# A graph-attention kernel: a second tile for drained products, spreading in nine groups, and another order of loads at each layer's start

## What is computed

```python
f_ni, f_nj, f_fij = nf @ W_ni, nf @ W_nj, ef @ W_fij
f_out = leaky_relu(f_ni[src] + f_nj[dst] + f_fij + bias, 0.2).reshape(-1, H, D)
e = einsum('ehd,hd->eh', f_out, attn)
emax = segment_max(e, dst)
a = exp(e - emax[dst]); a = a / segment_sum(a, dst)[dst]
h = (nf @ W_node).reshape(-1, H, D)
h_out = segment_sum(h[src] * a[:, :, None], dst)
nf, ef = h_out.mean(axis=1), f_out.mean(axis=1)
```

## Time and profile before

| | us |
|---|---|
| median of three runs | 3715.75 |
| lowest and highest run | 3714.92, 3718.35 |
| the profiled execution, its own time | 3716.28 |
| its span, first to last instruction | 3714.5 |
| PE busy | 2692.3 (72%) |
| DVE busy | 2424.4 (65%) |
| POOL busy | 1891.6 (51%) |
| ACT busy | 1634.7 (44%) |

### The profile page before, as it was taken

The page is one execution under the profiler, slowest core; times in us unless marked ns, Lnnn a source line. Parts: engine busy times, 40 slices in busy tenths (PEclk is TensorE's granted clock), DMA queues, the critical chain, the costliest instruction groups (busy, mean ns, idle before and its releaser), DMA issues.

```text
span 3714.5 us, 54737 instructions
## 1 busy us (share of the span) xinstructions
PE 2692.3 (72%) x18232; PEld 2153.1 (58%) x18259; DVE 2424.4 (65%) x5843; ACT 1634.7 (44%) x4133; POOL 1891.6 (51%) x1987
## 2 busy tenths in 40 slices
PE   3477777768677458777777777856777787777885
PEld 2465656656565256566666656536666666666653
DVE  6376767767768536676676767753667576676775
ACT  0144544544445315454454545532444444444453
POOL 5544554554553266455554545446555454554543
PEclk8787777777879778787777878868777777777776
DMA  6244334434342334343434433233343333433322
GB/s 218 86 122 137 120 122 144 128 126 133 122 130 88 121 107 119 115 137 114 147 120 134 126 115 122 98 107 110 100 121 119 112 108 105 123 114 114 95 81 84
DMA packets 149064, 440.48 MB, mean 119 GB/s; under 512 B 40892, under 2 KB 80672, under 8 KB 129977
## 3 DMA queue, kind: packets, MB, share of 16 engines
q1 hardware_dynamic: 82746, 385.31, 29.4%
q0 software_dynamic: 63200, 36.75, 7.1%
q10 hardware_dynamic: 2838, 14.91, 1.0%
HBM read 191.89 MB, written 244.95 MB: 118 GB/s over the span
## 4 chain that ended last, share of the span: by engine, by line
DVE 36%; PE 36%; issue 13%; ACT 9%; DMA 4%; POOL 2%; DVEq 0%; ACTq 0%; SPq 0%; POOLq 0%
DVE U L1465 15%; PE pick_ps L732 14%; PE f_ps L764 11%; PE f_ps L773 5%; DVE U L1450 4%; ACT f_low L919 4%; DVE rows L1386 4%; PE xT_ps L754 4%; DVE lr L1397 4%; DVE rows L1491 3%; ACT xT L910 2%; DMA z<-hot_tab 1%; ACT pick_sb L973 1%; DVE z L1477 1%; DVE mx_sc L1421 1%
## 5 line engine op out<-in xcount | busy, mean ns | idle before, releaser
L615 POOL DMA_INDIRECT rows<-nf_tab,src_sb x1815 | 1721.8, 949 | 1505.0 <-PE xT_ps L754 669.6
L732 PE MATMUL pick_ps<-nf_part,z 125*128 125x160 bf16 x9045 | 926.1, 270 | 578.9 <-ACT pick_sb L973 446.4
L732 PEld LDWEIGHTS pick_ps<-nf_part,z 125*128 125x128 bf16 x9045 | 835.1, 115 | 624.4 <-issue 459.9
L1397 DVE TENSOR_TENSOR lr<-f_ps,f_low 128x512 f32<-128x512 f32 x606 | 413.3, 682 | 930.7 <-ACT f_low L919 930.5
L773 PEld LDWEIGHTS f_ps<-w_out,lr 128*128 128x128 f32 x4836 | 721.4, 215 | 396.4 <-issue 296.7
L764 PE MATMUL f_ps<-xT,w_edge 97*128 97x512 f32 x1212 | 804.5, 752 | 70.2 <-ACT ef_new L941 47.2
L1465 DVE TENSOR_TENSOR_SCAN U<-wide_ps,U 128x272 f32<-128x272 f32 (+2 forms) x1272 | 801.9, 694 | 3.0 <-ACT wide_ps L982 1.9
L773 PE MATMUL f_ps<-w_out,lr 128*128 128x36 f32 (+1 forms) x4836 | 663.7, 278 | 30.2 <-DVE lr L1397 27.8
L919 ACT ACTIVATE f_low<-f_ps 128x512 f32<-128x512 f32 x606 | 360.6, 595 | 652.8 <-PE f_ps L764 652.5
L754 PE MATMUL xT_ps<-ident,rows 128*97 128x128 f32 x2418 | 449.9, 314 | 170.9 <-DVE rows L1386 141.8
L754 PEld LDWEIGHTS xT_ps<-ident,rows 128*97 128x97 f32 x2418 | 330.0, 186 | 188.5 <-DVE rows L1386 146.9
(11 more groups left out here) (164 smaller groups left out, 1215.4 us busy)
## 6 DMA issues: line engine op xcount, KB each, us to landing
u_tab<-up SPq DMA_DIRECT2D x144, 1088.0 KB, 5.0
z<-hot_tab SPq DMA_DIRECT2D x134, 468.8 KB
s_nd<-edge_first SPq DMA_DIRECT2D x48, 768.0 KB, 7.1
hot_tab<-z SPq DMA_DIRECT2D x67, 468.8 KB
rows<-nf_tab,src_sb POOLq DMA_INDIRECT x1815, 3.5
ef_tab<-ef_new SPq DMA_DIRECT2D x32, 768.0 KB, 4.1
ef_st<-ef_tab SPq DMA_DIRECT2D x32, 768.0 KB
edge_first<-s_nd ACTq DMA_DIRECT2D x16, 768.0 KB, 11.3
```

Source lines behind the costliest of these rows:

```text
L615: eng.indirect_dma_start(rows[q % RING][:, c * K:c * K + D], None, nf_tab[:, :], bass.IndirectOffsetOnAxis(ap=src_sb[:, t:t + 1], axis=0)) ...
L732: mm = eng.matmul(pick_ps[:, i * PB:(i + 1) * PB], hot[m % HOTS][0:NQ, f * PW + i * P:f * PW + (i + 1) * P], nf_part[a][0:NQ, f * PB:(f + ...
L1397: eng.tensor_tensor(lr[y][:, 0:w], f_ps[n % 2][:, 0:w], f_low[y][:, 0:w], ALU.max).then_inc(lr_ready, 1)
```

## The change

There are four edits.

1. `pick_sb` is gone. The four other candidates are drained alternately into two tiles that exist already, `m_spread` and `jw`, which are used at the end of each layer (and before the first). The drain of batch m waits for the selection of batch m-2 instead of m-1.
2. `SPREAD0` and `SPREAD` have nine entries instead of ten, with the same sum of 32.
3. At a layer's start SP issues its loads in another order. In the first layer ten `bring` stand in front of the first two row loads instead of four; in the others seven `bring`, the first row load, two `bring`, the second row load, where both row loads came after the seven. DVE does `slice_b(0)` and the first super-block's scans after the sixth `pick_rows` instead of the ninth in the second and third layer; in the first layer they stay behind the ninth.
4. In the fourth step of a sub-block ACT does `widen(k, 3)` after `lower(g+1)` instead of before `take_xT(g+2)`.

```diff
-SPREAD0 = (2, 5, 3, 3, 2, 5, 3, 3, 2, 4)
-SPREAD = (4, 4, 3, 2, 4, 4, 2, 2, 4, 3)
+SPREAD0 = (2, 5, 3, 3, 3, 5, 4, 4, 3)
+SPREAD = (4, 4, 3, 3, 4, 4, 3, 3, 4)
...
-        pick_sb = sb("pick_sb", [P, PICK * (PB - D)])
-        rest4 = pick_sb[:, :].rearrange("p (c b d) -> p c b d", b=PARTS5 - 1, d=D)
+        rest4 = [a[:, 0:PICK * (PB - D)].rearrange("p (c b d) -> p c b d", b=PARTS5 - 1, d=D)
+                 for a in (m_spread, jw)]
...
-                    loaded = START - 2 if l else IDXB + 2
+                    loaded = START - 2 if l else START + 1
                     for b in range(loaded):
                         bring(l, b)
                     load_first(q0)
+                    if l:
+                        for b in range(loaded, START):
+                            bring(l, b)
+                        loaded = START
                     load_first(q0 + 1)
...
-                        if m:
-                            eng.wait_ge(picked, (PARTS5 - 1) * m)
-                        eng.activation(rest4, pick4[:, :, 1:PARTS5, :], ACT.Copy
+                        if m >= 2:
+                            eng.wait_ge(picked, (PARTS5 - 1) * (m - 1))
+                        eng.activation(rest4[m % 2], pick4[:, :, 1:PARTS5, :], ACT.Copy
                                        ).then_inc(drained, 1)
...
                             widen(k, 2)
-                            widen(k, 3)
                         take_xT(g + 2)
                         if g + 1 >= 0:
                             lower(g + 1)
+                        if mine and i == 3:
+                            widen(k, 3)
...
-                                rest4[:, :, v - 1, :]).then_inc(picked, 1)
+                                rest4[m % 2][:, :, v - 1, :]).then_inc(picked, 1)
...
                         pick_rows(b)
-                    slice_b(0)
-                    spread_dst(0, range(D))
+                        if b == (START - 4 if l else START - 1):
+                            slice_b(0)
+                            spread_dst(0, range(D))
```

## The result

The changed kernel takes 2962.26 us, median of four runs (2954.03 to 2975.50), against 3715.34 us for the kernel before on the same chip: a ratio of 0.7975, 95% interval 0.7945 to 0.8006. The profiled execution took 2954.03 us. The forecast was 3000 us, 1.3% too long.

A forecast was written before the change was run, and what follows sets the result against it. The prediction took no single engine as the bound: DVE, PE and ACT wait for each other in turn. From 3716.3 us it took 147.5, 243 and 246.5 (rounds), 21 (spreading waits) and 59 (heads), giving 3000 us, range 2900 to 3100.

The forecast's parts named there:

- 14 rounds of layer 0: Layer 0's round falls from 67.04 to 56.5 us, keeping 3.9 us of one-hot stall and 2.5 us in the group after.
- lone spreading wait, three layers: Behind the 14 rounds of each layer, one more wait for spreading goes: some 7 us each, 21 in all.
- head of layer 0: Fifth-table loads ahead of the row loads let layer 0's spreading start 31 us earlier, between bounds of 18 and 33.
- heads of layers 1 and 2: Earlier spreading ends PE's 9.72 us idle before the first transpose; worth 14 us a layer, 28 for two.
- Layers 1 and 2: Rounds fall from 64.85 to 47.5 us in layer 1 and from 66.60 to 49 us in layer 2, with its lower clock.
- Spreading in nine groups: Scans end a group earlier, so PE's transpose at group 10 loses its 3.36 us wait; the cover is thin.
- The widening: Fourth-head widening moved behind lower on ACT: DVE's 0.86 us gap before the leaky, in up to three groups a round, goes.
- Nothing in the waits' place: Rival: layers 1 and 2 come down to the gathers' 45.0 us a round, layer 0 to 53; 2860 us, 12 in 100.
- New wait of the old kind: Rival: PE idles at one more place each round and a 5.11 us gap returns; 3215 us, 14 in 100.
- Gathers as the bound through the port: Rival: POOL's gathers, slowed beside DVE, need 53.3 us a round in layers 1 and 2; 3140 us, 6 in 100.
- The change does not do what it says: Rival: drains stay late because ACT comes late; only heads and lone spreading waits are won; 3636 us, 3 in 100.
- Clock at the low level throughout: Rival: PE idles in many small pieces and its clock stays low, rounds 75.7 us (79.6 in layer 0); 4110 us, 3 in 100.

The follow-up runs named there:

- the wide scores: Changed kernel with 36 columns instead of 4 in each score matmul of the last layer, the extra ones unread: 0.7896 of the kernel before, 2934.79 us.
- the eight groups: Changed kernel with the 32 scans of spreading in eight groups of a round instead of nine: 0.7941 of the kernel before, 2954.93 us.
- the best combination: Changed kernel with layer 0's third one-hots a group earlier, layer 2's scans in eight groups, six idle matmuls before group 6's product: 2889.44 us, 0.7774 of before.

## Why the prediction was right, and where it was off

Forecast and measured saving, term by term, in the profiled executions:

| term | forecast | measured |
|---|---|---|
| 14 rounds of layer 0 | 147.5 | 172.8 |
| 14 rounds of layer 1 | 243 | 253.0 |
| 14 rounds of layer 2 | 246.5 | 253.3 |
| lone spreading wait, three layers | 21 | 21.3 |
| head of layer 0 | 31 | 28.2 |
| heads of layers 1 and 2 | 28 | 12.8 + 17.0 |
| elsewhere | 0 | 3.9 |
| sum | 717 | 762.3 |

**The bound** was read rightly: the waits, not an engine. The drain's waits were removed whole, and the two tiles alone bring 367 us.

**Layer 0 is the term that was mis-sized**, by 25 of the 45 us. The stall itself was right: 3.9 us forecast, 4.05 measured, at the same product and for the same one-hots. The step that was off is the 2.5 us for the group after it (PE at the low level, without the spreading wait). The row shows 0.45 us there, 0.75 in the mean of the 14 rounds: the product itself runs at the low level (2.18 us), but the next leaky hardly feels it. The old spreading, put back, gives a mean gap of 5.6 us there, so most of that gap belongs to the spreading wait and its own low clock. The split within a round varies: with the wide scores, which leave layer 0 as it is, the mean there is 1.44 us, and all of DVE's idle time before its leaky is 5.8 us a round in both. Of the 7.2 us forecast in all, 1.4 did not come. DVE's own work, 48.9 us a round instead of 49.3, adds 0.4 us, which makes the 1.8 us by which the round is shorter than forecast.

**Layers 1 and 2** came within 0.7 and 0.5 us a round. In layer 1 DVE's own work is 44.28 us (654.89 - 34.9, over 14), not 44.75, and its waits are 2.5 us, not 2.75. Their places were half right: 1.1 us behind the product of group 6 (forecast 0.6), 0.9 in front of the leaky of group 11 and 0.5 at group 12 (forecast 1.4 in groups 9 and 10 and 0.75 unplaced). Layer 2 was held to be slower for its clock, and the wide scores bear that out for the most part.

**Spreading in nine groups.** "The wait goes" was too much: 14.9 us of it remain in layer 1, about 1 us a round, and the eight groups that end it bring no gain there. That "the cover is thin" was right.

**The widening** was counted as gaps of 0.86 us in up to three groups; its undoing costs 3.1 to 3.8 us a round, in layer 1 some 2.1 by those gaps and part of the rest by a late drain and PE's clock, a path that the prediction did not name. The sum did not suffer, because it was not made by adding up the parts: the rounds were forecast from what is left (DVE's work plus the residue). The undone parts cost 370, 255, 149 and 56 us, 830 together, while the whole change brought 753: a stall that returns alone costs more than it does beside the others, and an addition of single effects would have been 77 us out, where the forecast's sum was 45 out. The second tile is not the cause: it brings 367 us as the first of the edits and 370 as the last. The overlap lies among the other three (385 us together, 460 one by one); which of them share it was not tried.

**Heads.** Layer 0 came out between its two bounds (33 and 18), near the first. The one-hots waited 1.6 to 5.2 us for their loads, 18.9 us over seven sets. The row loads go out at 123.03, not at 120.11; with the 7.1 us of the earlier trace rows they would be there at about 130.1, an estimate, and DVE comes from its last selection at 130.90 (129.68 + 1.22). So the one-hots' chain and the loads end together. In layers 1 and 2 the 9.72 us are gone, as forecast. About half of the difference between the layers (12.8, 17.0) is product 7: it waits 2.64 and 2.79 us, but then takes 4.78 us in layer 1, where it took 4.64, and 3.29 in layer 2, where it took 5.34. The other half is the first product of each head: 5.92 us in layer 1, where it took 4.82, and 5.04 in layer 2, where it took 5.90.

**The rivals.** *Nothing in the waits' place* would have been 2860 us; it was nearest, and the best combination comes to 2889. *New wait of the old kind* did not come. *Gathers as the bound through the port* did not come: 947 ns each in a round that is a quarter shorter, as in the earlier trace rows. The rule of the Trainium skill quoted for it ("SBUF — State Buffer", "Who interferes with whom") is not contradicted, but no run here shows it acting on these gathers, even where POOL works almost without rest. Layer 0's gathers, in a stretch with 275 tensor_scalar of the one-hots, take 948 ns each. What it fits are scatters: in the kernel before, the one after that of 1.18 us runs beside a second cast and takes 1.34 us, where the median of the 75 is 0.99. *The change does not do what it says* did not come: the drain's waits are gone. *Clock at the low level throughout* did not come: layer 1 is at 0.95.

**The signs.** Of the signs named, those on the drain (now L977), on layer 1's clock and on the start of layer 0's spreading were met. DVE's idle time was met roughly: 2.5 and 4.1 us a round, for 3 to 4, and 5.8 in layer 0, for about 7. The transposes' was met in part. POOL's was badly put: its busy share is 0.74 in layer 1 (485.81 of 654.89), since the records leave out the time between two gathers (148.7 us); with it, it is 0.97.

## What to carry to other kernels

When engines wait for each other in turn, forecast a round from what stays (the busiest engine's own work plus the waits that remain), not by adding the prices of the removed waits; some of the prices depend on each other (830 us one by one, 753 together). A wait of PE has two prices, its length and the clock behind it: idle matmuls inside the wait show the second alone, and can win it where the wait can't be removed. After a stall is gone, look for the next one by the same row (idle time before one line) in each layer apart; here moving one set of one-hots by one group was worth 43 us more. A single row of a timeline shows that a stall can happen; how often it does takes all rounds.

## What the runs showed of the hardware

The clock after a wait of PE is not told by that wait's length alone. In the heads, waits of 0.81 us between products leave them at 3.27 us, one after another; a wait of 2.64 us is followed by a product of 4.78 us in layer 1, and one of 2.79 us by 3.29 us in layer 2, behind the same run of products. In the rounds the same 1.88 us before the product of group 6 is followed by either level:

```profile
1333.80 1.20 PE L736 MATMUL pick_ps<-nf_part,z 125*128 125x160 bf16 x15 [1.88 <-ACT jw L977]
...
2662.60 2.16 PE L732 MATMUL pick_ps<-nf_part,z 125*128 125x160 bf16 x15 [1.88 <-ACT pick_sb L973]
```

The first row is from layer 1 of the changed kernel, where the product takes 1.20 us in 11 rounds of 13 and 2.16 in two; in its layer 2 the count is the same. The second is from layer 2 of the kernel before, where it takes about 2.16 us in all 13. The granted clock of the three stretches is 0.95, 0.91 and 0.74, so the low level behind this wait is commoner where the clock is lower throughout; what decides it in a single round stays open.

More columns for the same count of matmuls made PE's busy time shorter, 602.68 against 621.59 us, by the clock (0.94 against 0.91).
